# Sorted experts of layer 0: scratch rows grouped by partition over eight tiles, zeroing in 1 MB pieces, and seven weight slots

## The reference

```
scores = sigmoid(x @ gate_w.T)              # 1024 tokens x 64 experts
# 4 of 8 groups of experts, then the best 8 experts in them
topk_w = scores[topk_idx]; topk_w = 2.5 * topk_w / sum(topk_w)
rw = zeros(1024, 64).at[token, topk_idx].add(topk_w)
expert_out[e] = silu(x @ Wg[e].T) * (x @ Wu[e].T) @ Wd[e].T     # hidden width 176
out = einsum('eth,te->th', expert_out, rw) + shared_mlp(x)
```

## Time and profile before

| | us |
|---|---|
| median of 3 runs | 4732.93 |
| the profiled execution, its own time | 4725.66 |
| its span in the profile | 4723.8 |
| cross-attention of layer 0, first to last context load | 29.89 to 683.64 |
| expert stage, scatter begins | 996.31 |
| first and last result copy of the tile loop | 1123.4 and 1517.7 |
| first gather | 1521.5 |

### The profile page before, as it was taken

The page is one execution under the profiler, slowest core; times in us unless marked ns, Lnnn a source line. Parts: engine busy times, 40 slices in busy tenths (PEclk is TensorE's granted clock), DMA queues, the critical chain, the costliest instruction groups (busy, mean ns, idle before and its releaser), DMA issues. The chain is left out here.

```text
span 4723.8 us, 142340 instructions
## 1 busy us (share of the span) xinstructions
PE 3939.4 (83%) x64206; PEld 3082.2 (65%) x64206; DVE 2213.5 (47%) x4094; ACT 1767.2 (37%) x3675; POOL 679.2 (14%) x392
## 2 busy tenths in 40 slices
PE   7999997636887299999975889999962689999988
PEld 5777775524655178888843567778742668887865
DVE  4545554523333455555554345555525155555533
ACT  3444453201111144444422334545431244444431
POOL 1111110140000411111031011111103011111100
PEclk9999998668999599999987899999975899999988
DMA  2222110025887311111031111111011711111100
GB/s 89 88 75 72 37 37 12 7 96 174 268 284 227 103 38 38 39 40 45 18 82 28 31 50 37 44 37 37 31 26 60 256 53 38 42 42 38 32 10 31
DMA packets 149222, 329.92 MB, mean 70 GB/s; under 512 B 31536, under 2 KB 104128, under 8 KB 145904
## 3 DMA queue, kind: packets, MB, share of 16 engines
q1 hardware_dynamic: 138976, 299.21, 19.9%
q0 software_dynamic: 6912, 18.88, 1.3%
q10 hardware_dynamic: 2736, 2.75, 0.2%
HBM read 261.67 MB, written 50.74 MB: 66 GB/s over the span
## 5 line engine op out<-in xcount | busy, mean ns | idle before, releaser
L654 DVE TENSOR_REDUCE x_pm<-banks 128x4 f32<-128x1536 f32 (+2 forms) x512 | 935.5, 1827 | 697.4 <-PE banks L555 697.4
L756 ACT ACTIVATE x_pl<-banks 128x384 f32<-128x384 f32 x1536 | 628.9, 497 | 730.9 <-PE banks L538 730.8
L480 POOL TENSOR_TENSOR x_cl<-xnT,x_ch 128x1601 fp32r<-128x1601 f32 x116 | 386.1, 3329 | 2197.4 <-ACT x_ch L771 2197.4
L761 ACT ACTIVATE x_kT<-banks,x_bk 128x384 f32<-128x384 f32 (+2 forms) x512 | 305.5, 597 | 535.9 <-PE banks L566 535.9
L578 PE MATMUL banks<-x_wh,x_ch 128*128 128x256 f32 (+1 forms) x1664 | 490.2, 295 | 0.0
L538 PE MATMUL banks<-x_q,x_kT 32*128 32x128 f32 x13312 | 484.7, 277 | 5.1 <-issue 4.6
L555 PE MATMUL banks<-x_kT,x_q 32*128 32x384 f32 (+2 forms) x4096 | 461.2, 515 | 13.4 <-DVE x_v L686 8.9
L578 PE MATMUL banks<-x_wh,x_cl 128*128 128x256 f32 (+1 forms) x1664 | 468.7, 282 | 1.4 <-issue 1.4
L578 PE MATMUL banks<-x_wl,x_ch 128*128 128x256 f32 (+1 forms) x1664 | 467.4, 281 | 0.0
L566 PE MATMUL banks<-x_ch,x_wh 128*128 128x384 f32 (+2 forms) x1024 | 410.9, 401 | 45.4 <-DVE x_cl L737 44.2
L538 PEld LDWEIGHTS banks<-x_q,x_kT 32*128 32x128 f32 x13312 | 438.5, 186 | 8.5 <-issue 6.0
(11 more groups left out here) (361 smaller groups left out, 5499.2 us busy)
## 6 DMA issues: line engine op xcount, KB each, us to landing
xnT<-in_ctxT SPq DMA_DIRECT2D x120, 800.5 KB, 4.4
e_w<-in_L_pack SPq DMA_DIRECT2D x127, 608.0 KB
e_w<-in_L_pack SPq DMA_DIRECT2D x21, 1154.0 KB
routed_y<-e_y SPq DMA_DIRECT2D x31, 512.0 KB, 5.8
e_xt<-routed_x SPq DMA_DIRECT2D x15, 1024.0 KB, 7.9
routed_x<-zero SPq DMA_DIRECT2D x7, 2048.0 KB, 11.7
a_swap<-a_raw SPq DMA_DIRECT2D x64, 128.0 KB, 2.3
actT<-in_ctxT SPq DMA_DIRECT2D x8, 800.5 KB, 4.5
```

What stands on the lines that cost most here:

```text
L480: nc.gpsimd.tensor_tensor(cl[:, u, k, 0:CTX], staged(b, k), ch[:, u, k, 0:CTX], ALU.subtract).then_inc(low_done, 1)
L654: nc.vector.tensor_reduce(pm[:, c, :, g], src[:, :, 0:hi - lo], AX.X, ALU.max).then_inc(max_done, 1)
L756: nc.scalar.activation(probabilities(c, j, lo, hi).rearrange("p t q -> p (t q)"), mine[j][:, 0:(hi - lo) * P], ACT.Exp).then_inc(exp_done, 1)
L761: nc.scalar.activation(kT[:, c, lo:hi], mine[1 if g == 0 and inside(b if c else b - 1) else 0][:, 0:hi - lo], ACT.Identity, bias=col[:, c: ...
```

## The change

1. The scratch tensors `routed_x` and `routed_y` are cut into groups of 8 tiles. Within a group the row of slot p of tile j stands at p * 8 + j, where it stood at j * 128 + p. A load of 8 tiles then reads 8 KB in one run for each partition instead of 8 runs of 1 KB; a store of 4 tiles writes runs of 4 KB. The tensors have 128 tiles instead of 127.
2. The slot numbers are turned into these row numbers by five more DVE instructions in the chain ahead of the scatter.
3. The zeroing goes in 16 DMAs of 1 MB instead of 8 (seven of 2 MB, one of 1920 KB), from a tile of 128 x 2048 zeros (8 KB runs), spread over the 14 steps b = 0 to 13, with two in the steps 6 and 13. POOL sets this tile to zero at the start of the stage, SP waits once for it; the old tile of zeros and its DVE memset go.
4. `SLOTS` is 7 instead of 5.

```diff
-    SLOTS = 5
+    SLOTS = 7
...
+        def grouped(rows):
+            return rows.rearrange("(g p j) n -> g p j n", p=P, j=LOAD)
...
             def load_rows(n):
-                tiles = tiles_of(n, LOAD)
-                rows = x_rows[tiles.start * P:tiles.stop * P, :].rearrange("(j p) n -> p j n", p=P)
-                sp.dma_start(xt[:, n % X_RING, 0:len(tiles)], rows).then_inc(x_in[n % X_RING], 16)
+                sp.dma_start(xt[:, n % X_RING], grouped(x_rows)[n]).then_inc(x_in[n % X_RING], 16)
...
                 if j == tiles.stop - 1:
-                    rows = y_rows[tiles.start * P:tiles.stop * P, :].rearrange("(j p) n -> p j n", p=P)
-                    sp.dma_start(rows, y[:, n % Y_RING, 0:len(tiles)]).then_inc(stored[n % Y_RING], 16)
+                    at = tiles.start % LOAD
+                    rows = grouped(y_rows)[j // LOAD][:, at:at + STORE]
+                    sp.dma_start(rows, y[:, n % Y_RING]).then_inc(stored[n % Y_RING], 16)
...
-            nc.vector.tensor_scalar(slot_i[:], slot[:].rearrange("p t k -> p (t k)"), -1.0, None, ALU.add).then_inc(slots_known, 1)
+            link(nc.vector.tensor_scalar(spot_i[:, 0], slot[:].rearrange("p t k -> p (t k)"), -1.0, None, ALU.add))
+            link(nc.vector.tensor_scalar(spot_i[:, 1], spot_i[:, 0], P - 1, 3, ALU.bitwise_and, ALU.logical_shift_left))
+            link(nc.vector.tensor_scalar(spot_i[:, 2], spot_i[:, 0], 7, LOAD - 1, ALU.logical_shift_right, ALU.bitwise_and))
+            link(nc.vector.tensor_scalar(spot_i[:, 3], spot_i[:, 0], LOADS * LOAD * P - LOAD * P, None, ALU.bitwise_and))
+            link(nc.vector.tensor_tensor(spot_i[:, 1], spot_i[:, 1], spot_i[:, 2], ALU.bitwise_or))
+            nc.vector.tensor_tensor(slot_i[:], spot_i[:, 1], spot_i[:, 3], ALU.bitwise_or).then_inc(slots_known, 1)
...
# cross_attention, SP
+            if clear is not None:
+                sp.wait_ge(zero_set, 1)
...
-                if clear is not None and b < CLEARS:
-                    rows = clear[b * CLEAR_TILES * P:min(b * CLEAR_TILES + CLEAR_TILES, ROUTED_TILES) * P, :]
-                    rows = rows.rearrange("(j p) n -> p j n", p=P)
-                    sp.dma_start(rows, spread(net.zero[:].unsqueeze(1), (P, rows.shape[1], D))).then_inc(net.cleared, 16)
+                if clear is not None:
+                    for n in range(b * CLEARS // (B - 2), (b + 1) * CLEARS // (B - 2)):
+                        rows = clear[n * CLEAR_TILES * P:(n + 1) * CLEAR_TILES * P, :].rearrange("(p j) n -> p (j n)", p=P)
+                        sp.dma_start(rows, zero[:]).then_inc(net.cleared, 16)
# cross_attention, POOL, ahead of its first work
+            if clear is not None:
+                nc.gpsimd.memset(zero[:], 0.0).then_inc(zero_set, 1)
...
-CLEAR_TILES = 16
+CLEAR_TILES = 8
```

More of the change, by code:

```diff
@@ L71, in __init__ @@
         self.next_count = 0
-        self.zero = self.sb("zero", [P, D])
         self.cleared = nc.alloc_semaphore("cleared")
@@ L124, in _ @@
             nc.vector.memset(net.ones[:], 1.0).then_inc(eps_set, 1)
-            nc.vector.memset(net.zero[:], 0.0).then_inc(eps_set, 1)
-            dve.wait_ge(eps_set, 3)
+            dve.wait_ge(eps_set, 2)
 def norm(net, tag, src, gamma, beta, ahead):
@@ L353, in cross_attention @@
     EARLY = GROUPS[0][1]
-    names = ("wv_in bias_in raw_in0 raw_in1 wk_high wk_low wv_high wv_low high_done low_done pad_set mask_in0 mask_in1 side_set shift_set "
+    names = ("wv_in bias_in raw_in0 raw_in1 wk_high wk_low wv_high wv_low high_done low_done pad_set mask_in0 mask_in1 zero_set side_set shift_set "
              "sums_set q_staged m_full max_done z_step z_ready z_turned nm_ready s_full exp_done k_full k_taken v_full "
@@ L358, in cross_attention @@
             block, wv_in, bias_in, raw_in0, raw_in1, wk_high, wk_low, wv_high, wv_low, high_done, low_done, pad_set, mask_in0, mask_in1,
-            side_set, shift_set, sums_set, q_staged, m_full, max_done, z_step, z_ready, z_turned, nm_ready, s_full,
+            zero_set, side_set, shift_set, sums_set, q_staged, m_full, max_done, z_step, z_ready, z_turned, nm_ready, s_full,
             exp_done, k_full, k_taken, v_full, v_taken, pv_full, o_taken, den_full, inverted, out_ready):
@@ L382, in cross_attention @@
         sets = [[net.bank(4 * n + j) for j in range(4)] for n in range(2)]
+        zero = net.sb(tag + "_zero", [P, CLEAR_TILES * D], ctx=mem) if clear is not None else None
         raw_v = early_p[:, 0].rearrange("p j t q -> p (j t q)")[:, 0:KC * D].rearrange("p (c f) -> p c f", c=KC)
@@ L1427, in routed_experts @@
         slot = net.sb(tag + "_slot", [P, TILES, K], ctx=mem)
+        spot_i = net.sb(tag + "_spoti", [P, 4, TILES * K], I32, ctx=mem)
         slot_i = net.sb(tag + "_sloti", [P, TILES * K], I32, ctx=mem)
@@ L2422, in program @@
         scratch = nc.dram_tensor("heads_scratch", (B, HEADS, S, 16), F32, kind="Internal").ap()
-        routed_x, routed_y = (nc.dram_tensor(n, (ROUTED_TILES * P, D), F32, kind="Internal").ap()
+        routed_x, routed_y = (nc.dram_tensor(n, (CLEARS * CLEAR_TILES * P, D), F32, kind="Internal").ap()
                               for n in ("routed_x", "routed_y"))
```

## The result

The changed kernel took 4672.85 us (median of 4 runs, 4665.56 to 4680.71) beside 4731.73 for the kernel before; the ratio is 0.9879, with a 95% interval of 0.9853 to 0.9906. It is 1.2% faster: a small gain, but the interval stays clear of 1. The forecast was 4649.5, in a range of 4622 to 4692.

What follows compares the result with a forecast made beforehand. It took late weight DMAs to hold the expert tile loop above PE's own pace. Loop -77, chain +1.2, last store +0.4 and zeroing -8 gave -83.4 us, from 4732.9 to 4649.5 us, range 4622 to 4692.

Steps and rivals of the forecast that it cites:

- The slots: Expert tile loop: 7 slots let weights arrive in time, 3.13 to 2.52 us a tile, a gain of 77 us.
- Rival B: Expert tile loop: DMA engines become the bound, 2.65 to 2.74 us a tile, gain 54 us, total 4672; chance 0.17.
- Rival D: Expert tile loop: slots don't help, 271 GB/s is the mix's limit, loop near 3.13 us a tile, total 4725; chance 0.05.
- The grouped rows: Row loads in the expert loop: 0 to 0.1 us of DMA time a tile, off the path, nothing for the sum.
- The chain: Five added instructions ahead of the scatter: all on the path, +1.2 us (1.0 to 1.6 if integer forms are slower).
- The zeroing: Layer 0's cross-attention: stall by bytes, 20 us as now, the clock's 11 us mostly gone; -8 us.
- rival C: Cross-attention: zeroing costs 3.9 us per event in 14 steps, 24 us more, total 4681; chance 0.12.
- The reading behind it: Cross-attention: PE's "issue" wait of 2.5 us during a zeroing read as instructions fetched late behind the zeros.
- The last store: On the way to the gather: last store is 512 instead of 384 KB, +0.4 us.
- Rival E: Scatter and gather: rows 8 KB apart slow them; at 2.0 us each, total 4743; chance 0.03.
- A: Whole kernel: expert loop at PE's pace, zeroing as now or cheaper, total 4625 to 4665; chance 0.63.

Runs made afterwards that it cites:

- e4: The kernel before with 7 weight slots instead of 5, 1 KB runs and old zeroing kept; ratio to before 0.9833, loop 313.8 us.
- e3: The changed kernel with 5 weight slots instead of 7, so without the added slots; ratio to before 1.0069, loop 397.3 us.
- e11: The kernel before with 6 slots and the zeroing in 14 steps in the middle of the half step; loop 349.2 us.
- e2: The changed kernel with the zeroing issued in the middle of the half step, not right behind the context load; ratio to before 0.9775, 43.5 us a step.
- e7: The changed kernel with 256 KB of each step's zeroing right behind the context load, the rest in the middle of the half step; 44.2 us a step.
- e10: The changed kernel with 512 KB of each step's zeroing right behind the context load, the rest in the middle of the half step; 45.6 us a step.
- e8: The kernel before with 7 slots and the zeroing in 14 steps in the middle of the half step, no grouped rows; ratio to before 0.9762.
- e1: The changed kernel with the zeroing as it was, 8 DMAs of 2 MB in 1 KB runs in steps 0 to 7; ratio to before 0.9852.
- e9: The changed kernel with the zeroing in the middle of the half step, plus an unused 1 MB load behind each context load; 45.8 us a step.
- e12: The changed kernel measured again, nothing altered; ratio to before 0.9908, 47.7 us a step.

## Why the prediction was right, and where it was off

- **The slots: right.** 3.13 to 2.52 us a tile and 77 us were forecast; 2.51 and 78.0 came. The reason given (2.8 to 3.8 us between issue and use against the 5.1 to 8.0 us a load takes) is shown by e4 and e3, and e11 adds the point in between, with late tiles just behind the row loads. Rival B fell: DMA held 337 GB/s and its engines were 94% booked, but nothing waited for long. What stood for it, that the loop "never held more than 263 to 271 GB/s", was a mean and no limit. The 249 ns of a weight packet did include waiting that isn't capacity: in the stretch of the earlier trace rows the median of these packets is 187 ns, and those that began in the first 0.3 us after the queue had been empty for over 0.1 us took 619 ns in the mean; in the changed loop (1155 to 1465), where it was never empty that long, the mean is 225 ns. Rival D fell too.
- **The grouped rows: right** in bringing nothing to the loop (e3 against before, e4 against after).
- **The chain: right.** 1.2 us were forecast. In the changed kernel its first instruction starts at 1020.46 and the last at 1021.63, 1.17 us apart:

```profile
1020.46 0.20 DVE L1615 TENSOR_SCALAR e_spoti<-e_slot 128x64 int32<-128x64 f32 x1
1020.69 0.20 DVE L1616 TENSOR_SCALAR e_spoti<-e_spoti 128x64 int32<-128x64 int32 x1
...
1021.63 0.23 DVE L1620 TENSOR_TENSOR e_sloti<-e_spoti 128x64 int32<-128x64 int32 x1
```

- **The zeroing: this is the step that failed.** It was seen that a zeroing of 2 MB costs 3.9 us, and "I take the stall by bytes ... with the clock's 8 x 1.4 = 11 us mostly gone" gave -8 us. What came is what rival C named: 4.1 us for each step with a zeroing, 47.6 us a step (the prediction's own sign of C was 47.5), +21.7 us in the 13 steps and most of another 3 us behind the last load, where step 13 issues its two. That is 25 against the 24 of C, and 33 us off the term. Both halves of the step were wrong. The stall was to stay at 20 us; beyond the waits that e2 has too, it rose from 18.8 to 32.0 us in the 13 steps. The clock's share was to fall from 11 us to some 3; it rose from 12 to 24 us, half of the time at a granted clock of 0.50. The split of the 3.9 us into 2.5 and 1.4, with the clock's part read from the 0.65 shortly after a zeroing against the 1.00 without one, was right (18.8 and 12 us over 8 steps are 2.4 and 1.5). The rows had a single size of zeroing and could not tell bytes from events, so 0.12 for C was too low. e7, e10 and the table show why half the bytes didn't help: above 1 MB the fetch lands no later.
- **The reading behind it: right.** That PE's instructions are fetched late behind the zeros was a guess from a wait with no engine. The q8 packets show it: in the changed kernel the first fetch behind a context load lands after 7.6 us, in e2 after 4.8, and the waits end 1.2 to 1.6 us after a landing. It costs where PE issues 30 and more matmuls per us, and nothing when the same DMAs are moved 9 us (e2).
- **The last store: right** (last copy to first gather 3.8 us before, 4.0 now). **Rival E fell**: the scatter took 80.0 us before and 79.9 now, the gather 79.1 and 78.9.
- The sum: -83.4 us were forecast, and the two spans differ by -47.0. Of the 36 us between, 33 are the zeroing, 5 are the other entries of the ledger (+0.5, +2.5, +2.1, which hardly any term covered), and the loop gave 1 back. The medians differ by 59, so against them the miss is 23 us; that these 12 us came in the forecast's favour is the spread of single executions, and luck. The low end of A, 4625, is about 4732.9 - 77 + 1.6 - 31, a zeroing that costs nothing; no run shows that right behind the context load, where 1 MB cost 3.9 to 5.1 us, and e2 shows it only 9 us later. The range held because it had been stretched to C, a case that was given 0.12, and not because the way to 4649.5 was right.

## What to carry over

Ring depth is worth working out as time: slots ahead times the consumer's pace, less the issue delay, against the longest landing time of a load with the big transfers in front of it. Here the sixth slot was worth 45 us and the seventh some 33, until that reached 8 us, and bigger packets nothing. A transfer that nobody waits for still had a price here where PE went through its instructions fastest (4.1 us a step for 1 MB of zeros, and none 9 us later): compare the same loop with and without it, look when the packets of the instruction queue land beside an "issue" wait, and try another place before another size.

## What the runs showed of the hardware

- By size the late fetch and what follows cost 0.7 us a step (256 KB), 2.1 (512 KB), 3.9 to 5.1 (1 MB), 3.6 to 5.5 (2 MB), and nothing 9 us later in the same loop. In the changed kernel 32 us of this were stalls and 24 us a granted clock of 0.50 from about the end of some of them. In e2, e7, e8 and e11, whose waits come to 8.6 to 14.5 us, the granted clock stayed at 1.00.
- The DMA share of 94 to 97% over 300 us, at 337 GB/s, went with waits of 6 to 8 us in all: a high share by itself didn't make DMA the bound of this loop.
- While POOL issues the 64 scatters, the shared units took a different time from group to group for the same code: from first scatter to first result 101 to 102 us in e1 to e8, all on one chip, and 127 to 130 in the first measurement and in e9 to e12. These 26 us are most of the 35 us by which the kernel before differed between the first measurement and e1 to e4.
